# A two-layer decoder on one core: the two sequences' stages interleaved in another order

## The reference: what is computed

```
x = x + L0_attn(LN(x))           # 32 heads of 64, 8 key/value heads, RoPE, window 32, a sink per head
x = x + L0_xattn(LN(x), ctx)     # 16 heads of 16, q and k with RMS norm
x = x + L0_ffn(LN(x))            # softmax router, top 8 of 64, sum of weighted biases
x = x + L1_attn(LN(x))           # 32 query heads on 8 key/value heads of 8, plus a memory part
x = x + L1_xattn(LN(x), ctx)     # scores summed over the batch, |.| and max(.,1), group norm, gate
x = x + L1_ffn(LN(x))            # top 2 of 8 experts, silu(gate) * up, down
```

## Time and profile before

| what | value |
|---|---|
| timed runs | 1836.09, 1837.38, 1838.32 us; median 1837.38 |
| the profiled execution | 1832.11 us |
| its span in the trace | 1830.3 us |
| mean granted clock of PE | 0.789 |
| first start of 1:l0 / last stages of the first part | 34.7 us / about 1466 us |

### The profile page before, as it was taken

How to read it: one execution, slowest core, us unless ns; L and a number is a source line. 1 busy time by engine, 2 the same in 40 slices (tenths; PEclk the granted TensorE clock), 3 DMA queues, 4 the chain that set the end, 5 groups by cost and what they waited for, 6 DMA issues and landing times.

```text
span 1830.3 us, 37451 instructions
## 1 busy us (share of the span) xinstructions
PE 1352.7 (74%) x14566; PEld 1024.7 (56%) x14566; DVE 1266.0 (69%) x2529; ACT 657.9 (36%) x1533; POOL 224.3 (12%) x375
## 2 busy tenths in 40 slices
...
DMA packets 51245, 70.82 MB, mean 39 GB/s; under 512 B 4912, under 2 KB 46576, under 8 KB 49520
## 3 DMA queue, kind: packets, MB, share of 16 engines
...
## 4 chain that ended last, share of the span: by engine, by line
issue 66%; PE 15%; DVE 8%; POOL 4%; ACT 3%; DMA 2%; POOLq 0%; SPq 0%; DVEq 0%; ACTq 0%
PE ps L900 11%; POOL rstd L1337 3%; POOL rstd L1336 1%; DMA out<-ptf 1%; PE ps L904 1%; DVE experts L675 1%; PE ps L472 1%; ACT big L1256 1%; PE ps L1002 1%; DMA ptf<-in_spread 1%; PE ps L398 1%; DVE ptf L1509 1%; ACT experts L517 0%; PE ps L445 0%; DMA kf<-in_dn 0%
## 5 line engine op out<-in xcount | busy, mean ns | idle before, releaser
L1256 ACT ACTIVATE big<-ps,st 128x128 f32<-128x128 f32 x768 | 205.6, 407 | 205.6 <-DVE st L1590 205.6
L1002 PE MATMUL ps<-ident,big 128*128 128x128 f32 x1024 | 183.7, 347 | 34.6 <-ACT big L1256 18.3
L1509 DVE TENSOR_TENSOR ptf<-ps,ptf 128x1024 f16<-128x1024 f32 x128 | 154.4, 1221 | 64.7 <-ACT ptf L1262 63.4
L1002 PEld LDWEIGHTS ps<-ident,big 128*128 128x128 f32 x1024 | 163.0, 185 | 61.4 <-ACT big L1256 31.7
L1336 POOL TENSOR_TENSOR rstd<-mv,eps 128x1 f32<-128x1 f32 x80 | 18.4, 229 | 1274.4 <-DVE mv L1400 1274.4
L1262 ACT ACTIVATE ptf<-ps 128x1024 f16<-128x1024 f32 x128 | 130.6, 1031 | 88.9 <-PE ps L1002 88.8
L1588 DVE TENSOR_REDUCE st<-ps 128x8 f32<-128x1024 f32 x96 | 117.0, 1218 | 35.5 <-PE ps L900 35.5
L900 PE MATMUL ps<-wo,qhl 128*128 128x256 f32 x512 | 119.6, 388 | 15.4 <-DVE qhl L1514 13.2
L900 PEld LDWEIGHTS ps<-wo,qhl 128*128 128x128 f32 x512 | 96.0, 192 | 32.9 <-issue 15.2
L900 PE MATMUL ps<-experts,ptf 128*128 x312 | 100.4, 383 | 0.0
L1242 ACT ACTIVATE qhl<-big 128x1024 f16<-128x1024 f32 x32 | 33.8, 1057 | 162.9 <-DVE big L1474 160.6
...
## 6 DMA issues: line engine op xcount, KB each, us to landing
...
```

Of the source, the lines that this page charges most:

```text
L1002: m = pe.transpose(ps_f(u, j // 4, P, (j % 4) * P), big[u][:, j * P:(j + 1) * P], ident[:])
L1256: m = f(big[u][:, c], ps_all[u][:, c], ACT.Exp, scale=scale, bias=st32[u][:, 3, j:j + 1])
L1509: S(u, tt(pt_l[u][:, c], ps_all[u][:, c], pt_h[u][:, c], ALU.subtract), f"pt{n}l{h}")
```

## The change

The texts of the four engines are replaced by others. No stage, wait or buffer changes, `FIRST` stays as it is, and so do SP's program and the second part. With the lists unrolled over the turns, each sequence's own stages stand in the same order in both kernels, on every engine. What differs is how sequence 0's are interleaved with sequence 1's, and where each list is cut:

- PE: 1:a3m and 1:a30 to 1:a33 now stand together ahead of 0:a20. Behind them come 0:a20, 0:a21, 0:a22, 1:T00, 0:a23, 1:T01, 1:a50 to 1:a53, 1:a60, and only then 0:a3m and 0:a30 to 0:a33, and 1:a61. Before, 0:a3m to 0:a33 stood ahead of 1:T00. Further on, items of sequence 0 have moved ahead of their neighbours of sequence 1 by one or two places: 0:pv1 ahead of 1:pk3, 0:atr ahead of 1:memp, 0:prj ahead of 1:c3a0, 0:a17 ahead of 1:pv3a, 0:tr3 ahead of 1:c3b1, 0:pk3 ahead of 1:pv3b, 0:c3a0 ahead of 1:tr4; and 1:a0 of the next turn ahead of 0:pv3a.
- DVE: 1:q1 stands ahead of 0:a32v and 0:l0; 1:q2 to 1:ql1 ahead of 0:k0; all of 1:s00, 1:s01, 1:n00, 1:n01, 1:l00 ahead of 0:q1, and 1:l01, 1:o0b, 1:o0d between the items 0:q1 to 0:q3. 0:l00 stands ahead of 1:a6v, 1:l10 and 1:l11 ahead of 0:a6v, 0:l10 ahead of 1:a19e, 0:a11 ahead of 1:pk3v, 0:a12 ahead of 1:mv, 0:a13 ahead of 1:s3a0, 0:n2 ahead of 1:s3a1, 0:xT3 ahead of 1:s3b0, 0:a19e ahead of 1:l3b0, 0:pk3v ahead of 1:a22b, 0:mv ahead of 1:n4.
- ACT: 0:qh0 and 0:qh1 behind 1:e00 to 1:o0c; 0:h00 ahead of 1:kvm; 0:a19s ahead of 1:h3b0.
- POOL: the unrolled order is the same.
- The cuts. PE: before between 1:a60 and 1:a61, now between 1:pv3az and 1:c3b0. DVE: before between 0:n0 and 0:a0v, now between 1:a19e and 0:l11. ACT: before between 1:e3a0 and 1:e3a1, now between 1:e11 and 1:h10. POOL: before between 1:pk and 1:pq, now between 0:rs1 and 0:pk. The start, ahead of the loop, is longer by as much.

The diff, without the texts of the removed lines' middle part:

```
 TENSOR_TURN = """
-1:a61 1:kv1 0:T00 1:tr1 0:T01 1:a7 0:a50 0:a51 1:pkk 0:a52 0:a53 1:pk1 0:a60 1:c10 1:c11 0:a61 1:T10 1:T11
...
-0:mx1 0:mx2 1+a22 0+a0 1+a23 0+a1a 0+a1b 0+a1c 0+a20 0+a21 1+a3m 1+a30 1+a31 0+a22 0+a23 1+a32 1+a33 0+a3m
-0+a30 0+a31 0+a32 0+a33 1+T00 1+T01 1+a50 1+a51 1+a52 1+a53 1+a60
+1:c3b0 0:tr3 1:c3b1 0:a19 1:T3b0 1:T3b1 0:pk3 1:pv3b 1:pv3bz 0:memp 0:c3a0 1:tr4 0:c3a1 1:mx1 1:mx2 0:T3a0
+0:T3a1 1+a0 0:pv3a 0:pv3az 0:c3b0 0:c3b1 1+a1a 1+a1b 0:T3b0 0:T3b1 1+a1c 0:pv3b 0:pv3bz 1+a20 1+a21 0:tr4
+0:mx1 0:mx2 1+a22 0+a0 1+a23 0+a1a 0+a1b 0+a1c 1+a3m 1+a30 1+a31 1+a32 1+a33 0+a20 0+a21 0+a22 1+T00 0+a23
+1+T01 1+a50 1+a51 1+a52 1+a53 1+a60 0+a3m 0+a30 0+a31 0+a32 0+a33 1+a61 0+T00 1+kv1 0+T01 0+a50 1+tr1 0+a51
+1+a7 1+pkk 0+a52 0+a53 1+pk1 0+a60 1+c10 1+c11 0+a61 1+T10 1+T11 0+kv1 1+pv1 1+pv1z 0+tr1 1+atr 1+prj 0+a7
+0+pkk 1+tr2 1+a15 0+pk1 0+c10 1+a16 0+c11 1+a17 1+tr3 1+a19 0+T10 0+T11 0+pv1 1+pk3 0+pv1z 0+atr 1+memp 0+prj
+1+c3a0 1+c3a1 0+tr2 0+a15 1+T3a0 1+T3a1 0+a16 0+a17 1+pv3a 1+pv3az
 """
 SCALAR_TURN = """
-1:e3a1 0:a15s 1:h3a0 1:h3a1 1:e3b0 1:e3b1 1:h3b0 1:h3b1 0:a19s 0:qT3 1:a31s 0:e3a0 0:e3a1 0:h3a0 0:h3a1 1+a0s
...
+1:h10 1:h11 0:kvm 0:rk 0:rq 1:a15s 0:qT1 0:e10 0:e11 0:h10 1:a19s 0:h11 1:qT3 1:e3a0 1:e3a1 0:a15s 1:h3a0
...
 VECTOR_TURN = """
-0:a0v 1:q1 0:k0 1:q2 1:q3 1:q4 1:ql0 1:ql1 0:v0 0:k0l 0:q1 1:s00 0:q2 0:q3 0:q4 0:ql0 0:ql1 1:s01 1:n00 1:n01
-1:l00 1:l01 0:s00 1:o0b 1:o0d 0:s01 0:n00 0:n01 1:a6v 1:kvv 1:n1 1:kvp 1:xT1 0:l00 0:l01 1:a7k 1:a7v 1:a8
...
+0:l11 0:a11 1:pk3v 0:a12 1:mv 0:a13 1:s3a0 0:n2 1:s3a1 0:xT2 0:a15v 0:a15t 1:l3a0 0:a16v 1:l3a1 0:a17v 1:a22a
+0:n3 0:xT3 1:s3b0 1:s3b1 0:a19v 0:a19e 1:l3b0 1:l3b1 0:pk3v 1:a22b 0:mv 1:n4 1:xT4 0:s3a0 0:s3a1 1:a32v 1+l0
+1+n0 0:l3a0 0:l3a1 0:a22a 1+a0v 0:s3b0 0:s3b1 1+k0 0:l3b0 0:l3b1 0:a22b 1+v0 0:n4 1+k0l 0:xT4 1+q1 0:a32v 0+l0
+0+n0 0+a0v 1+q2 1+q3 1+q4 1+ql0 1+ql1 0+k0 0+v0 0+k0l 1+s00 1+s01 1+n00 1+n01 1+l00 0+q1 1+l01 0+q2 1+o0b
+1+o0d 0+q3 0+q4 0+ql0 0+ql1 0+s00 0+s01 0+n00 0+n01 0+l00 1+a6v 1+kvv 1+n1 1+kvp 1+xT1 1+a7k 0+l01 1+a7v 1+a8
+1+a7q 0+o0b 0+o0d 1+s10 1+s11 1+l10 1+l11 0+a6v 0+kvv 0+n1 0+kvp 1+a11 0+xT1 1+a12 0+a7k 1+a13 0+a7v 1+n2 0+a8
+1+xT2 0+a7q 1+a15v 1+a15t 1+a16v 1+a17v 0+s10 1+n3 1+xT3 0+s11 1+a19v 0+l10 1+a19e
```

More of the change, by code:

```diff
@@ L98 @@
+1+a7 1+pkk 0+a52 0+a53 1+pk1 0+a60 1+c10 1+c11 0+a61 1+T10 1+T11 0+kv1 1+pv1 1+pv1z 0+tr1 1+atr 1+prj 0+a7
+0+pkk 1+tr2 1+a15 0+pk1 0+c10 1+a16 0+c11 1+a17 1+tr3 1+a19 0+T10 0+T11 0+pv1 1+pk3 0+pv1z 0+atr 1+memp 0+prj
+1+c3a0 1+c3a1 0+tr2 0+a15 1+T3a0 1+T3a1 0+a16 0+a17 1+pv3a 1+pv3az
 """
 SCALAR_TURN = """
-1:e3a1 0:a15s 1:h3a0 1:h3a1 1:e3b0 1:e3b1 1:h3b0 1:h3b1 0:a19s 0:qT3 1:a31s 0:e3a0 0:e3a1 0:h3a0 0:h3a1 1+a0s
-0:e3b0 0:e3b1 0:h3b0 0:h3b1 1+v0h 1+k0h 0:a31s 0+a0s 1+qh0 1+qh1 0+v0h 0+k0h 0+qh0 0+qh1 1+e00 1+e01 1+h00
```

12 lines of the change are left out of this document (4 added, 8 removed).

## The result

The kernel after takes 1877.55 us (median of four runs, 1872.47 to 1880.38), the one before 1837.07 (four runs, 1836.09 to 1838.32). The ratio is 1.0217, with a 95% interval from 1.0193 to 1.0241: 40 us more. The profiled execution of after took 1872.47 us, its span is 1870.7, and the mean granted clock of PE is 0.794. I had said 1872.

A forecast was written before the change was run, and what follows sets the result against it. No engine is full; hand-over waits in the longest walk through four engine lists set a turn's cost. Terms 8.4 + 9 + 0 + 16.8 = 34 us on 1832.1 gave 1866, plus 5.3 for the median: 1872, range 1845 to 1888.

The forecast's parts named there:

- DVE's cut: Loop branch on DVE, moved ahead of 0:l11: 2.7 us exposed instead of 1.3, +1.4 us a turn, +8.4 us.
- PE's cut: Loop branch on PE, moved ahead of 1:c3b0: 1.5 us a turn newly exposed, +9 us.
- order in the layer-0 stretch: Sequence 1 through 1:a60 ahead of 0:a3m: gains and new waits sum to 0, bounds -3 and +2 us a turn.
- order behind it: Moves behind the layer-0 stretch: together 2.1 us a turn, over eight turns +16.8 us.
- (a): 1:l10 and 1:l11 ahead of 0:a6v on DVE: 0:a6v's 1.2 us come behind them, +1.2 us a turn.
- Rival 3: PE's clock still at 1.2 GHz in 1:a60, 0:s00 waits: 15 us on top, 1887, or 30, 1902; chance 0.14.
- (b): 0:a11, 0:a12, 0:a13 ahead of 1:pk3v, 1:mv, 1:s3a0, and 0:prj ahead of 1:c3a0: +0.6 us a turn, bounds 0 and 2.
- (c): 0:tr3 and 0:xT3 ahead of 1:c3b1 and 1:s3b0: +0.3 us a turn, bounds 0 and 1.6.

The follow-up runs named there:

- experiment 1: The kernel before, old order, with only DVE's list cut at the new place: 1844.77 us, ratio 1.0047.
- experiment 2: The kernel before, old order, with only PE's list cut at the new place, between 1:pv3az and 1:c3b0: 1852.69 us, ratio 1.0084.
- experiment 5: The kernel before, old cuts, with only the layer-0 stretch of the new order: 1844.05 us, ratio 1.004.
- experiment 6: The kernel before, old cuts, with the new order only behind layer 0: 1846.69 us, ratio 1.0054.
- experiment 11: The kernel before with only 1:l10 and 1:l11 put ahead of 0:a6v on DVE: 1849.98 us, ratio 1.0059.
- experiment 8: The kernel before, old order, with only DVE's list cut ahead of 1:s10 instead of ahead of 0:a0v: 1832.13 us, ratio 0.9969.
- experiment 3: The kernel before, old order, with all four engines' lists cut at the new places: 1857.47 us, ratio 1.0119.

## Why the prediction was right

1872 was forecast and 1877.6 measured, with the sign and the size right. The sum is better than its terms:

| step | forecast, us | measured |
|---|---|---|
| DVE's cut | +8.4 | +8.6 (5.9 to 11.6), experiment 1 |
| PE's cut | +9 (0 to 11) | +15.4 (11.9 to 18.9), experiment 2 |
| order in the layer-0 stretch | 0 (-24 to +16) | +7.3 (3.9 to 10.8), experiment 5 |
| order behind it | +16.8 | +9.9 (6.8 to 13.0), experiment 6 |
| of it, step (a) | +9.6 | +10.8 (8.3 to 13.2), experiment 11 |
| whole change | +34 | +40 (35 to 44) |

- **DVE's cut** was right by its mechanism and its size: 2.61 us of issue ahead of 0:l11, and 1.2 less ahead of 0:a0v. Ahead of a wait of 3.83 us the same branch adds nothing (experiment 8). The Trainium skill ("Runtime: NRT & Kernel Launch", "Instruction fetch mechanics") says that a taken branch to a target outside the two fetched pages waits until that page is there. The trace agrees on DVE (experiment 1) and on PE (experiment 2); on ACT there is nothing of the kind, where the next instruction of after starts 0.07 us behind the begin of the branch, taken or not.
- **PE's cut** was mis-sized: its upper bound of 11 us lies below the measured interval. I subtracted the last stage ahead of it (0.75 us) as cover, and PE's idle time shows little of it: 3.05 to 3.48 us in experiment 2. Beyond the 2.2 us a turn that then remain, 15.4 / 6 = 2.6 were measured; what the other 0.4 is made of isn't settled.
- **The layer-0 stretch** was right as a walk: 1:l01's gap shrank, 0:s00 waits 1.04 us (I had 1.1), and a turn at full clock is as long as before (experiment 5). The term failed in that it priced a turn at one clock. Rival 3 was this mechanism, and it came true in some turns: in turns 0, 6 and 7 of after 1:a60 took 2.0 to 2.4 us more, and the wait ahead of 0:s00 grew by 1.9 to 2.4; what rival 3 didn't have is 0:a60, which took 1.5 to 1.7 us more in the same turns, and with it 1:s10's wait.
- **Behind it**, (a) was right. For (b) and (c), 0.9 us a turn, nothing shows within the noise; they were not run by themselves.
- **The parts don't add.** The two halves of the order cost 7.3 and 9.9 alone and 10.3 together; cuts and order cost 21.8 and 10.3 apart and 40 together; both gaps, 7 and 8 us, are just clear of the noise. The profiles of experiment 3 and of after (15.8 us apart) show a part of the reason. Turns 1 to 5 are equal (181.2 and 181.0 us on average): there the new order costs nothing on top of the cuts. Turns 0, 6 and 7 are 5.0, 3.2 and 3.0 us longer in after (172.9, 184.0, 207.0 against 167.9, 180.8, 204.0), 11.2 together, and they are those in which 1:a60 and 0:a60 ran partly at 1.2 GHz; in experiment 3 they took 3.7 us in each. Another 3.9 are in the second part (365.7 against 361.7), with its cause open.

Why (a) costs nothing in turns 1 to 5 of after can be read from 1:s10 and 0:s10, between which DVE's list differs from the old one in (a) alone. In turn 3 of experiment 3, whose 1:l0 starts at 565.37, they are:

```profile
663.30 1.23 DVE L1588 TENSOR_REDUCE st<-ps 128x8 f32<-128x1024 f32 x1 [3.83 <-PE ps L900]
...
689.53 1.19 DVE L1588 TENSOR_REDUCE st<-ps 128x8 f32<-128x1024 f32 x1
```

and in after, where 1:l0 starts at 571.26 and 1:s10 at 667.84, 0:s10 is

```profile
695.81 1.19 DVE L1588 TENSOR_REDUCE st<-ps 128x8 f32<-128x1024 f32 x1
```

So 1:s10 comes 97.9 us behind 1:l0 in experiment 3 and 96.6 in after, and 0:s10 124.2 and 124.6: the new order gains 1.3 us up to 1:s10 (1.3 to 1.9 in turns 1 to 5), and (a) takes them.

So the number was right in part by luck. Of the four terms one was right (DVE's cut). PE's cut was 6.4 us too low, the layer-0 stretch 7.3 too low and the order behind it 6.9 too high; two of these took each other away, and since the parts don't add, what is left can't be given to the third. The 5.6 us between 1872 and 1877.6 are less than what the turns with the low clock took (11.2).
